# Last block of a spiking feed-forward layer: spikes as one sign each, counted behind the products, three tiles of results added by DMA

## The reference

```python
h = square(relu(x @ W_fc.T))            # 1250 x 4096
y = h @ W_proj.T                        # 1250 x 1024
mem = 0                                  # five steps:
    reset = mem > 1
    mem   = 0.9 * mem + y - reset
    spk   = mem > 1                      # counted over the steps
out = x + count(spk) / 5
```

## Time and profile before

| what | value |
|---|---|
| median of three runs | 1630.81 us |
| the profiled execution | 1631.58 us |
| its span in the profile | 1629.6 us |
| PE busy | 1603.5 us (98%) |
| DVE busy | 894.4 us (55%) |
| ACT busy | 462.8 us (28%) |
| POOL busy | 97.9 us (6%) |
| last hidden products end, last projections begin | 1563.76 us |

### The profile page before, as it was taken

One profiled execution on the slowest core, in us unless ns is written; L12 is line 12 of the kernel. 1 busy time (PEld: TensorE's weight loads), 2 busy tenths in 40 slices (PEclk: granted clock), 3 DMA queues, 4 the chain that ended last, 5 costly groups with the idle time before them and its releaser, 6 DMA issues.

```text
span 1629.6 us, 22403 instructions
## 1 busy us (share of the span) xinstructions
PE 1603.5 (98%) x7709; PEld 1344.4 (83%) x7709; DVE 894.4 (55%) x1613; ACT 462.8 (28%) x816; POOL 97.9 (6%) x190
## 2 busy tenths in 40 slices
PE   7999999999999999999999999999999999999997
PEld 5777667788888888889899899898998888888884
DVE  7786777565212222656334343343443788888868
ACT  3344454211112000114123131130321333333358
POOL 0230134200000000001000000000001000000000
PEclk9999999999999999999999999999999999999998
DMA  7322333467533454558122021120223233333321
GB/s 296 133 104 82 115 114 130 178 246 261 186 103 121 186 206 159 180 194 287 50 78 78 26 103 51 51 103 26 77 69 111 104 116 116 116 116 116 116 91 49
DMA packets 55926, 205.43 MB, mean 126 GB/s; under 512 B 5330, under 2 KB 13852, under 8 KB 50340
## 3 DMA queue, kind: packets, MB, share of 16 engines
q1 hardware_dynamic: 53524, 191.76, 33.3%
q0 software_dynamic: 2320, 12.58, 2.0%
HBM read 153.85 MB, written 50.47 MB: 125 GB/s over the span
## 4 chain that ended last, share of the span: by engine, by line
PE 95%; issue 1%; DVE 1%; DMA 1%; ACT 1%; DVEq 0%; POOL 0%; SPq 0%; ACTq 0%; POOLq 0%
PE bank L1588 26%; PE bank L1569 26%; PE bank L1425 26%; PE bank L1518 11%; PE bank L1374 3%; PE bank L1401 2%; ACT spikes L900 1%; PE bank L1620 0%; DMA w_landing<-w_self 0%; DVE w L1079 0%; DMA pr_raw<-w_proj 0%; DMA at_dram<-counts_tile 0%; DMA rows<-x 0%; DVE key_hot L1026 0%; DVE xt L1067 0%
## 5 line engine op out<-in xcount | busy, mean ns | idle before, releaser
L1425 PE MATMUL bank<-w,xt 128*128 128x512 f32 x1920 | 462.7, 396 | 2.6 <-DVE w L1079 2.6
L1569 PE MATMUL bank<-x2t,fc_w 128*128 128x384 f32 (+1 forms) x2304 | 438.4, 350 | 0.4 <-ACT relu L865 0.4
L1569 PEld LDWEIGHTS bank<-x2t,fc_w 128*128 128x128 f32 x2304 | 411.7, 188 | 25.6 <-issue 0.7
L1425 PEld LDWEIGHTS bank<-w,xt 128*128 128x128 f32 x1920 | 356.8, 189 | 76.9 <-issue 3.3
L1588 PE MATMUL bank<-pr_w,hid 128*128 128x512 f32 (+1 forms) x1824 | 418.7, 390 | 0.0
L1588 PEld LDWEIGHTS bank<-pr_w,hid 128*128 128x128 f32 (+1 forms) x1824 | 338.2, 185 | 75.5
L1291 DVE TENSOR_TENSOR y<-y,bank 128x512 f32<-128x512 f32 (+1 forms) x152 | 104.2, 687 | 214.8 <-PE bank L1588 214.8
L1518 PE MATMUL bank<-z,at 128*128 128x512 f32 x800 | 186.9, 392 | 0.0
L1518 PEld LDWEIGHTS bank<-z,at 128*128 128x128 f32 x800 | 148.8, 188 | 30.2
L860 ACT ACTIVATE pr_w<-pr_raw 128x1024 fp32r<-128x1024 f32 x64 | 67.1, 1049 | 365.6 <-PE bank L1588 362.6
L1234 DVE TENSOR_TENSOR square<-relu 128x384 f32<-128x384 f32 (+1 forms) x96 | 56.9, 592 | 144.2 <-ACT relu L865 144.2
(11 more groups left out here) (127 smaller groups left out, 931.8 us busy)
## 6 DMA issues: line engine op xcount, KB each, us to landing
fc_raw<-w_fc SPq DMA_DIRECT2D x64, 512.0 KB, 4.3
pr_raw<-w_proj SPq DMA_DIRECT2D x64, 512.0 KB, 3.5
xt<-xt_dram SPq DMA_DIRECT2D x24, 1024.0 KB, 5.0
xt_dram<-xt SPq DMA_DIRECT2D x18, 1024.0 KB, 4.3
at<-at_dram SPq DMA_DIRECT2D x20, 640.0 KB, 5.9
part_dram<-rows SPq DMA_DIRECT2D x20, 512.0 KB, 3.8
rows<-part_dram SPq DMA_DIRECT2D x20, 512.0 KB, 4.5
rows<-x SPq DMA_DIRECT2D x18, 512.0 KB, 4.9
```

The source lines that it names most:

```text
L1425: ins = nc.tensor.matmul(bank[:, 2 * (u % 2) + q, :], xt[j][:, a, k, :], w[:, k, b, q * HALF:(q + 1) * HALF], start=(k == 0 and m == 0), s ...
L1569: ins = nc.tensor.matmul(bank[:, 4 + (c if g == 0 else j % 2), 0:n], fc_w[:, j % 2, k, a, :], x2t[g][:, k, v, c0:c0 + n], start=(k == 0 an ...
```

## The change

- **Pieces.** The last block's projection is a function of its own (`last_products`). All halves are projected one after the other, and the last half as two pieces of 256 columns: 9 pieces. The membrane steps of pieces 0 and 1 run 6 and 5 deep before the next piece's, the others 4 as before.
- **Spikes.** A spike of steps 1 to 4 is one `Sign` straight into bf16, +1 or -1, with a bias column `tie_col`. The first spike of a piece gets a second instruction, a relu with the bias 5 (`start_col`), so that the sum is twice the count; results scale by 0.1 in place of 0.2. The very last spike is made by DVE (`last_spike`, 0 or 2), its piece starting from 4.
- **Counting.** Half h is counted behind the products of half h + 3 (h up to 4), half 5 and all that follows behind the last product.
- **Results.** Of halves 0 to 5 ACT scales the count from PSUM into `y1` (`rates`), and POOL adds it to `out` by an accumulating DMA; a DMA from DRAM to DRAM has put x there early, at the start of the feed-forward layer. Only the last tile's x is loaded (0.5 MB in place of 2 MB), and only its three results run on DVE and are stored by SP.
- There are 25 spike slots instead of 13.

```diff
-SPIKE_SLOTS = 13
+SPIKE_SLOTS = 25
...
-        MEM_STAGES = [[(half - late, step + late * MEM_STEPS // 2) for step in range(MEM_STEPS // 2) for late in (0, 1)
-                       if 0 <= half - late < LAST_HALVES] for half in range(LAST_HALVES + 1)]
+        PIECES = [(half, 0, HALF) for half in range(LAST_HALVES - 1)]
+        PIECES += [(LAST_HALVES - 1, c, HALF // 2) for c in (0, HALF // 2)]
+        RATE_HALVES = LAST_HALVES - 2
+        FIRST_STEPS = [6, 5] + [4] * (len(PIECES) - 2)
+        MEM_STAGES = []
+        for p in range(len(PIECES) + 1):
+            new = [(p, step) for step in range(FIRST_STEPS[p])] if p < len(PIECES) else []
+            old = [(p - 1, step) for step in range(FIRST_STEPS[p - 1], MEM_STEPS)] if p > 0 else []
+            MEM_STAGES.append([entry for pair in itertools.zip_longest(new, old) for entry in pair if entry])
...
+        DVE_SPIKE = (len(PIECES) - 1, STEPS - 1)
+        SPIKE_STAGES = [[(p, 0)] * (p < len(PIECES)) + [(q, (step + 1) // 2) for q, step in stage if step % 2 == 1]
+                        for p, stage in enumerate(MEM_STAGES)]
+        SPIKE_ORDER = [entry for stage in SPIKE_STAGES for entry in stage if entry != DVE_SPIKE]
+        COUNT_STAGES = [[] for _ in PIECES]
+        for half in range(RATE_HALVES - 1):
+            COUNT_STAGES[half + 3] += [(half, s) for s in range(STEPS)]
+        COUNT_STAGES[-1] += [(RATE_HALVES - 1, s) for s in range(STEPS)]
+        COUNT_STAGES[-1] += [(p, s) for p, s in SPIKE_ORDER if p >= RATE_HALVES] + [DVE_SPIKE]
+        COUNT_ORDER = [entry for stage in COUNT_STAGES for entry in stage]
+        LAST_ADDED = Y_START + sum(ADDED) - LAST_HALVES
...
+        def proj_bank(p):
+            return p % 4 if p < LAST_HALVES else 0
+        def sum_of(p):
+            half, c, width = PIECES[p]
+            return bank[:, 4 + half % 4 if p < LAST_HALVES else 1, 0:width]
...
-                sp.dma_start(out[n * T:n * T + rows_of(n), c:c + HALF],
-                             half_of(x1_1, half)[0:rows_of(n), :]).then_inc(out_stored[1], 16)
+                c += half % 2 * HALF
+                sp.wait_ge(result_ready, done + 1)
+                sp.dma_start(out[n * T:n * T + rows_of(n), c:c + width],
+                             x1_last[0:rows_of(n), c:c + width]).then_inc(out_stored[1], 16)
             sp.wait_ge(out_stored[0], 16 * (n0 // T))
-            sp.wait_ge(out_stored[1], 16 * LAST_HALVES)
+            sp.wait_ge(out_added, 16 * RATE_HALVES)
+            sp.wait_ge(out_stored[1], 16 * (len(PIECES) - RATE_HALVES))
...
+            rated = slice(n0, n0 + RATE_HALVES // 2 * T)
+            pool.dma_start(out[rated, :], x1_dram[rated, :]).then_inc(out_prepared, 16)
+            nc.gpsimd.memset(tie_col[:, 0:1], -(1.5 + 2.0 ** -23)).then_inc(columns_ready, 1)
+            nc.gpsimd.memset(start_col[:, 0:1], float(STEPS)).then_inc(columns_ready, 1)
+            nc.gpsimd.memset(start_col[:, 1:2], float(STEPS - 1)).then_inc(columns_ready, 1)
...
-            pool.dma_start(x1_1[:, :, :], x1_tiled[:, n0 // T:, :]).then_inc(x1_in[1], 16)
+            pool.dma_start(x1_last[:, :], x1_tiled[:, TILES - 1, :]).then_inc(x1_in[1], 16)
+            pool.wait_ge(out_prepared, 16)
+            for half in range(RATE_HALVES):
+                n = n0 // T + half // 2
+                c = half % 2 * HALF
+                pool.wait_ge(rates_ready, half + 1)
+                pool.dma_start(out[n * T:(n + 1) * T, c:c + HALF], piece_of(y1, half),
+                               accum_op=ALU.add).then_inc(out_added, 16)
...
-                    act.wait_ge(spikes_counted, spike - SPIKE_SLOTS + 1)
-                nc.scalar.activation(spikes[:, spike % SPIKE_SLOTS, :], sign[:, spike % 2, :], ACT.Relu,
-                                     scale=-1.0).then_inc(spikes_ready, 1)
...
-                nc.scalar.activation(sign[:, spike % 2, :], source, ACT.Sign, bias=1.0, scale=-1.0).then_inc(signs, 1)
...
+                nc.scalar.activation(sign[:, 0:width] if start else spike_of(p, s), source, ACT.Sign, bias=tie_col[:, 0:1],
+                                     scale=1.5).then_inc(signs, 1)
+                if start:
+                    act.wait_ge(signs, spike + 1)
+                    constant = int(p == DVE_SPIKE[0])
+                    nc.scalar.activation(spike_of(p, s), sign[:, 0:width], ACT.Relu,
+                                         bias=start_col[:, constant:constant + 1]).then_inc(starts_ready, 1)
+            def rates(half):
+                act.wait_ge(spikes_counted, COUNT_ORDER.index((half, STEPS - 1)) + 1)
+                nc.scalar.activation(piece_of(y1, half), sum_of(half), ACT.Copy,
+                                     scale=0.5 / STEPS).then_inc(rates_ready, 1)
+            act.wait_ge(columns_ready, 3)
+            for p, stage in enumerate(SPIKE_STAGES):
+                for entry in stage:
+                    if entry != DVE_SPIKE:
+                        spike_sign(*entry)
+                if 0 <= p - 3 < RATE_HALVES:
+                    rates(p - 3)
...
-            def result(half):
+            def result(p):
                 dve.wait_ge(x1_in[1], 16)
-                dve.wait_ge(spikes_counted, SPIKE_ORDER.index((half, STEPS - 1)) + 1)
-                part = half_of(x1_1, half)
-                nc.vector.scalar_tensor_tensor(out=part, in0=bank[:, 4 + half % 4, :],
-                                               scalar=1.0 / STEPS, in1=part,
+                dve.wait_ge(spikes_counted, COUNT_ORDER.index((p, STEPS - 1)) + 1)
+                part = piece_of(x1_last, p)
+                nc.vector.scalar_tensor_tensor(out=part, in0=sum_of(p), scalar=0.5 / STEPS, in1=part,
                                                op0=ALU.mult, op1=ALU.add).then_inc(result_ready, 1)
-            for half, stage in enumerate(MEM_STAGES):
-                if half < LAST_HALVES:
-                    add_share(1, BLOCKS - 2, half // 2, halves=(half % 2,))
+            for p, stage in enumerate(MEM_STAGES):
+                if p < len(PIECES):
+                    add_piece(p)
                 for place, entry in enumerate(stage):
                     mem_step(*entry)
-                    if half >= 3 and place == 1:
-                        result(half - 3)
-            result(LAST_HALVES - 2)
-            result(LAST_HALVES - 1)
+                    if p == len(PIECES) and place == 0:
+                        result(RATE_HALVES)
+            dve.wait_ge(mem_steps, MEM_ORDER.index((DVE_SPIKE[0], 2 * DVE_SPIKE[1] - 1)) + 1)
+            nc.vector.tensor_scalar(last_spike[:, :], mem_of(DVE_SPIKE[0], DVE_SPIKE[1] - 1), THRESHOLD, 2.0, ALU.is_gt,
+                                    ALU.mult).then_inc(last_spike_ready, 1)
+            for p in range(RATE_HALVES + 1, len(PIECES)):
+                result(p)
...
+                if last:
+                    return
...
-                        if last:
-                            add_spikes(2 * n + q - 2)
...
+            def last_products():
+                length = 2 * BLOCK
+                first_hid = F_TILES * 3 - length
+                for p, (half, c, width) in enumerate(PIECES):
...
+                    pe.wait_ge(y_added, LAST_ADDED + p - 3)
+                    for j in range(length):
...
+                        for i, (a, v) in enumerate(PASSES):
+                            ins = nc.tensor.matmul(bank[0:height, proj_bank(p), 0:width],
+                                                   hid_of(1, j)[:, a, n * T:n * T + height],
+                                                   pr_of(j)[:, v, column:column + width],
+                                                   start=(j == 0 and i == 0), stop=(j == length - 1 and i == 2))
+                    ins.then_inc(proj_summed, 1)
+                    for entry in COUNT_STAGES[p]:
+                        add_spike(*entry)
...
+                if (p, s) == DVE_SPIKE:
+                    pe.wait_ge(last_spike_ready, 1)
+                elif s == 0:
+                    pe.wait_ge(starts_ready, p + 1)
+                else:
+                    pe.wait_ge(signs, SPIKE_ORDER.index((p, s)) + 1)
...
+                if s == 0 and 4 <= p < LAST_HALVES:
+                    pe.wait_ge(rates_ready, p - 3)
+                nc.tensor.matmul(sum_of(p), ident_narrow[:, :], spike_of(p, s), start=(s == 0),
+                                 stop=(s == STEPS - 1)).then_inc(spikes_counted, 1)
...
-            for stage in range(LAST_HALVES - 2, LAST_HALVES + 1):
-                add_spikes(stage)
+            last_products()
```

More of the change, by code:

```diff
@@ L1 @@
+import itertools
 from contextlib import ExitStack
@@ L331, in gnn_ffn @@
         LAST_HALVES = 2 * n1 // T
-        MEM_STAGES = [[(half - late, step + late * MEM_STEPS // 2) for step in range(MEM_STEPS // 2) for late in (0, 1)
-                       if 0 <= half - late < LAST_HALVES] for half in range(LAST_HALVES + 1)]
-        MEM_ORDER = [entry for stage in MEM_STAGES for entry in stage]
```

(53 more changed lines are left out.)

81 lines of the change are left out of this document (53 added, 28 removed).

## The result

Eight runs of the changed kernel gave 1625.27 to 1628.24 us, median 1626.28; eight of the kernel before, on the same chip, 1630.16 to 1632.55, median 1631.12. The ratio is 0.9972, 95% interval 0.9963 to 0.9982: faster by 4.6 us (4.8 by the two medians), where 4.8 were forecast. A second set of nine runs on another chip gave 1626.16 us and again 0.9972 (0.9962 to 0.9983). In the experiments one execution, the profiled one of e9_late_no_acc, took 2014.74 us at a mean granted clock of 0.745; it is left out of that run's median, and no profile of that kernel is read.

A forecast was written before the change was run, and what follows sets the result against it. PE was taken to bound the kernel until the last block, ACT there. With DVE as new bound the span ends at 1624.7, 4.9 less than 1629.6; 1630.81 - 4.8 gave 1626.0 us, range 1625.0 to 1629.2.

The forecast's parts named there:

- First sum at 1569.2: Last block: half 0's products are complete at 1569.2, so DVE starts 4.7 us earlier than 1574.02.
- Narrow products 3.1 us a piece: Last half on PE: products of 256 columns cost 0.13 us each, 3.1 us for the 24 of a piece.
- the second rival: Last half on PE: narrow products cost what wide ones do, piece 8 complete at 1618.3, median 1629.2; chance 0.07.
- ACT no longer the bound: Last block: ACT needs 4.4 us a half instead of 6.2, less than DVE.
- the fourth rival: Last block: ACT still bounds, sign behind sign without idle time, about 1627 us; chance 0.03.
- DVE as the bound: Last block: DVE, at 5.57 us a full stage, sets the end from half 6 on; its last result ends at 1621.7.
- The early copy at nothing: Start of the feed-forward layer: the 1.5 MB DRAM copy ends near 788 and costs nothing; without cover up to 11 us.
- The accumulation lands before the last store: End of span: the sixth accumulating DMA, issued at 1619.4, takes 4 us and ends 1.1 us before the other path.
- 2.8 us to the end: From the last result's end to the span's end 2.8 us pass as before, the halved store counted at nothing.
- the walk: Step-by-step timing of the last block through PE, ACT and DVE, ending the span at 1624.5 before a 0.2 us correction.
- The 0.2 I had added at the end: End of span: correction to 1624.7, since the same timing of the kernel before fell 0.5 us short of its trace.
- The slower rival: Accumulating DMAs do not keep up and run serially; at 7 us each the median is 1636; chance 0.05.

The follow-up runs named there:

- e9_late_no_acc: Changed kernel with the counts of halves 0 to 5 put behind pieces 6 to 8 and no accumulating DMAs: 1622.45 us, ratio 0.9948.
- e1_single: Kernel before, with only the first two halves of the last block projected one after the other: 1629.31 us, ratio 0.999.
- e3_two: Changed kernel with two ACT instructions for every spike again (sign to scratch, then relu or copy) and 24 slots: 1634.44 us, ratio 1.0023.
- e5_rates_dve: Changed kernel with the six copies of spike counts out of PSUM made by DVE instead of ACT: 1626.99 us, ratio 0.9979.
- e4_whole: Changed kernel with the last half as one piece of 512 columns: 1628.61 us, ratio 0.9984.
- e6_no_acc: Changed kernel without its six accumulating DMAs, the spike rates of halves 0 to 5 left out of the output: 1625.01 us, ratio 0.9968.
- e2_late: Changed kernel with halves 0 to 5 counted and copied behind pieces 6, 6, 7, 7, 8, 8: 1627.08 us, ratio 0.9973.
- e8_again: Repetition of e8_spread on one chip with the changed kernel: 1623.11 us, ratio 0.9956.
- e8_spread: Changed kernel with counts behind pieces 6, 6, 7, 7, 8, 8 and ACT's copies in stages 5, 5, 6, 6, 7, 7: 1623.35 us, ratio 0.9955.

## Why the prediction was right, and where it was off

The forecast was 1626.0 and the time 1626.28. By its steps, times of the forecast moved by the 1.35 us of the late start:

- **First sum at 1569.2 + 1.35 = 1570.6:** 1570.61. Half 6 at 1606.65: 1606.62. Half 6's sum is 1.74 us sooner in the tail than before (41.67 against 43.41), 1.8 forecast. In e1_single, with counts behind each half, it is 1.1 sooner and the end 1.7.
- **Narrow products 3.1 us a piece:** 2.99. PE never held the last pieces' sums, so the second rival (chance 0.07) is out; DVE took both without idle time.
- **ACT no longer the bound:** it idles in the stages of 512 columns (1.91 us in the half shown), and giving it a second instruction costs 7.9 us of tail (e3_two). But the sum priced a half of 512 columns only, 4.4 us. In the stage of piece 8 ACT works from 1617.12 to 1620.71 without idle time, level with DVE, and the profile's chain runs through it, close to the fourth rival (chance 0.03, "sign behind sign without idle time"). That DVE has no gap there (the sum of piece 8 comes 4.20 us behind that of piece 7, 4.22 forecast) shows that it cost nothing.
- **DVE as the bound, walked to a last result at 1621.3 + 1.35 = 1622.65:** 1622.67. Work added to DVE from half 6 on moves it one for one (e5_rates_dve, three copies of 0.6, 1.8 us), narrowing it helps (the split, 1.8 us in e4_whole, in which one piece also waits 0.98 us for PE).
- **The early copy at nothing:** it landed 15.8 us after its issue at 766.58, at 782.4 and so before the 788 of the forecast, and the products beside it are the same 32.68 and 33.30 us as in the earlier trace rows; no weight was late.
- **The accumulation lands before the last store, 4 us taken:** 4.0 in the median of the six, and SyncE's last wait is for the store. Issued at 1621.00, where 1619.4 + 1.35 was forecast.
- **2.8 us to the end, the halved store counted at nothing: this step failed in size.** Two things lie in it: without accumulations the end is 0.5 us shorter than before (2.26 in e6_no_acc against 2.79), for which the smaller store is the likely and untested reason, and the accumulations, of which I only asked whether the sixth ended later than the store, lengthen the end by 1.1. Together +0.6, the difference between 4.4 us saved in the last block and some 5 by the walk. The 0.2 I had added at the end hid a third of it.
- **The size of the gain:** the walk ended at 4.9 us and the forecast subtracted 4.8, which is rounding. The time before 1563 us has no steady shift: the two profiles of the changed kernel begin the last projections 1.35 us later and 1.0 sooner than before. That the medians lie 4.8 us apart, just as forecast, while the last block gained 4.4 is luck: the other 0.4 has no cause on record, and the interval runs from 2.9 to 6.0 us.

The slower rival was real in kind: e2_late shows accumulations that queue up and end last. The forecast had all six come 6.5 us apart. That is wrong for the last two by its own walk, in which the stages of pieces 7 and 8 take 4.22 and 3.14 us, and they came 4.2 and 3.0 apart. At some 2.2 us of busy DMA engines each they still kept up, so the rival stayed away. What is open: whether the store waits on the DMA engines or on memory while the accumulation is under way; no run tells these apart.

## What to carry to other kernels

When a transfer is "off the path" because it ends before the last one, ask also what it does to the last one while both move: here the accumulations added 1.1 us to the 2.3 behind the last result. And when a bound is lifted (counts out of PE's way, 3 us), look where the work that was spread out now lands together: the same six accumulations cost 1.1 us when the last two were issued 4.2 and 3.0 us behind the ones before them, and some 4 when issued in pairs at the end; making each copy a stage sooner kept the gain. Ask this of every engine that the shorter stages touch: ACT, taken as free, was level with DVE in the stage of 256 columns. Finally, walk the last block from the trace's own issue distances, dependent and independent ones apart: that placed the last result within 0.1 us here.

## What the runs showed of the hardware

- An accumulating DMA of 256 KB (128 rows of 2 KB, to DRAM) from POOL: 0.85 to 0.91 us of POOL for the issue, where a plain store of 512 KB in the same kernel has 0.54; 4.0 us to landing in the median of the changed kernel (the plain one 2.9), 5.0 to 5.5 where they are issued in pairs (e8_again, e8_spread, e2_late), and about 2.2 us of busy DMA engines each where six follow on end.
- A product of 256 columns with 98 weight columns costs 0.125 us and one of 512 columns 0.227: 0.55 of the time for half the columns.
- A copy of 1.5 MB from DRAM to DRAM behind a 4 MB load landed 14.9 to 16.6 us after its issue in the ten profiles read.
